# Two strips of counts in the third layer of a graph network, and 32 dense pairs with 40 gathered batches in its last two rounds

## The chip, the cores and the metric

The kernel runs on one core of one Trainium2 chip, in one launch. The metric is the device time of a launch in microseconds. Three runs of the kernel before took 5751.9, 5758.0 and 5763.0 us. The engines are named as in the profile: PE (matmuls), PEld (PE's loads of weights), DVE (vector), ACT (activation), POOL (GpSimd, which here issues the gathers of rows from DRAM) and SP (which issues the other transfers).

## The reference

Four graph layers follow each other on 6250 nodes of 128 features and one list of 106250 edges, sorted by the node `dst` that they end in; each layer adds its input and normalises the rows.

```python
x = ln(x + L0(x, src, dst, edge_type_16))   # two relational convolutions: means by (dst, relation), then a product
x = ln(x + L1(x, src, dst))                 # attention with a softmax over the edges of a node
x = ln(x + L2(x, src, dst, edge_type_8))    # below
x = ln(x + L3(x, src, dst))                 # below, twice

# L2: a relational layer, a residual product, and a norm over the nodes
agg = segment_sum(xW[src, etype], dst)
h = relu(agg + x @ loop_w + bias)
h = h + relu(x @ res_w + res_b)
out = (h - mean(h, 0)) * rsqrt(var(h, 0) + EPS) * bn_gamma + bn_beta

# L3: the mean of the neighbours, twice
def sage(x, W_l, W_r, b):
    return (segment_sum(x[src], dst) / max(degree, 1)) @ W_l.T + b + x @ W_r.T
out = sage(relu(sage(x, W1_l, W1_r, b1)), W2_l, W2_r, b2)
```

## The kernel before

The edges lie in 832 tiles of 128, and 8 tiles are a batch (104 batches). A round goes over all edges once: the first layer has two rounds, the second and third one each, the fourth two. In the gathering rounds POOL issues one indirect DMA for each tile, eight for a batch (`gather_near`, line 889, and `gather_mixed`, line 861), into a ring of four buffers. ACT copies the indices of a batch into one of four small buffers (`stage`, lines 1040 and 972); POOL waits for that copy, and ACT makes it when the batch four (in the last rounds three) before has been used.

The third layer's round (`near_round(near_c, ...)` on PE and DVE, `run_counting` on ACT) has 104 steps and one more, a batch each. In a step PE multiplies the gathered rows with one-hot matrices made by DVE (line 1491), ACT copies the sums out of PSUM (line 1065), PE multiplies them with the relations' weights one step later (line 1477), ACT copies again (line 1055), PE places the result (line 1501) and DVE adds it to the sums (line 2148).

Beside this the same round counts, for the fourth layer, how often each node is a source in each pair of batches. A pair d (0 to 29) is 16 tiles, of at most 128 target nodes; its counts are a strip of 128 partitions by 50 x 136 numbers in bf16, which is stored to DRAM (`neighbours`) when the pair is done. For a tile, DVE makes two one-hot matrices (lines 2023 for all of a step, 2029), PE multiplies them in two halves into two banks of PSUM (`count_tile`, line 1417), ACT takes them out into the strip at the tile's offset, all columns but the first (line 1034), and the first ones into a small buffer `SIDE` (line 1035), and DVE adds those to the strip (`correct`, line 2040). The banks are one set: PE begins a tile when ACT has taken out the one before. Five tiles are counted in a step (`PER`), three before and two beside the batch's own products; after 96 steps all pairs are counted. The loop's body is a lap of 16 steps, 5 pairs. There is one strip, `MADE_UP`. SP stores it when DVE's last correction is in (line 793), and ACT, before it takes out the first tile of the next pair, waits for that store:

```python
if j == 0:
    if not isinstance(d, int) or d > 0:
        act.wait_ge(made_out, d * 16)
```

The layer's residual product runs in the same round: 16 pieces of 400 columns, two in each lap and four behind the laps, a matmul (line 1702) and an activation into `H` (line 1266) each. After the round DVE waits for all of them (`res_act`) and goes on with `H`.

The last two rounds (`mixed_round`) use the counts. The first 60 batches, 30 pairs, are dense: SP loads a pair's strip into one of two buffers (line 798, when the products of the pair before the last are done), and PE multiplies it, 49 blocks of 128 nodes, with the rows of all nodes, held in SBUF as three bf16 parts (line 1710, 128x384 each); DVE adds up the three parts (line 2589), PE places the result (line 1756) and DVE adds it. The other 44 batches are gathered by POOL as before, and PE collects each in eight products (line 1780). The order of the work is written out: PE goes through half steps h, two for a pair (24 and 25 products), and a collect stands behind a half step that is a slot. Half steps 0 and 1 are the head, with a slot each; then a loop of four laps of 12 half steps (6 pairs), in which two of three half steps are slots (8 batches), and each half step also has a piece of the `x @ W_r` product (lines 1765, 1770); then the tail, 10 half steps (5 pairs), all of them slots. A pair whose tiles don't fit (more than 127 nodes in all, or steps from tile to tile above 11 nodes) takes another path, tile by tile (`wide`).

POOL issues the gathers in one loop from the moment the table of rows is stored, so ahead of PE by up to the ring's four buffers.

Of the kernel before, what the change touches and what calls it, by code (L numbers as in the profile page):

```python
# [22 lines left out]
ALU = mybir.AluOpType  # L23
# [59 lines left out]
def build(nc, a, out):  # L83
    ctx = ExitStack()
    with ctx:
# [237 lines left out]
        HOTS = PER  # L323
# [6 lines left out]
        MADE_UP = ROOM[:, 2 * NODES_P + R8 * P:2 * NODES_P + R8 * P + COUNTED].bitcast(BF16)  # L330
        MADE_HALVES = MADE_UP.rearrange("p (a h s) -> p a h s", a=2, s=STRIDE)
# [285 lines left out]
        def counted_in(lap, u):  # L617

            found = []
            for n in range(PER):  # L620
                q, j = divmod(PER * (u - 1) + n, PAIR)
                found.append((lap * PER + q, j))
            return found

        def offsets_of(engine, k):

            _, values = nc.values_load_multi_w_load_instructions(OFFSETS[0:1, bass.ds(k * PER - PER, PER)],
                                                                 engines=[engine.engine], min_val=0, max_val=LATEST,
                                                                 skip_runtime_bounds_check_because="VectorE clamps the offsets")
            return values  # L630
# [19 lines left out]
        def slot_before(lap, h):  # L650
# [4 lines left out]
            return lap * 2 + n // RING, n % RING  # L655

# [12 lines left out]
        def _(sp):  # L669
# [121 lines left out]
            with sp.Fori(0, DENSE) as d:  # L791
                sp.wait_ge(mx_cor, d * PAIR + PAIR)
                sp.dma_start(neighbours[bass.ds(d, 1), :, :].rearrange("o p s -> (o p) s"), MADE_UP).then_inc(made_out, 16)
# [139 lines left out]
        def _(act):  # L933
# [35 lines left out]
            def mixed_round(m, rows, final):  # L969
# [26 lines left out]
                with act.Fori(0, LAPS - 1) as lap:  # L996
# [20 lines left out]
            def take_out(d, j, n, offsets):  # L1017
# [13 lines left out]
                if j == 0:  # L1031
                    act.copy(MADE_HALVES[:, :, :, 0:SPAN], counted_of(2)).then_inc(mx_out, 1)
                else:
                    act.copy(MADE_HALVES[:, :, :, bass.ds(offsets[n] + 1, SPAN - 1)], counted_of(2)[:, :, :, 1:SPAN])  # L1034
                    act.copy(SIDE[:, n, :].rearrange("p (a h) -> p a h", a=2), counted_of(2)[:, :, :, 0]).then_inc(mx_out, 1)

            def near_round(r):
# [4 lines left out]
                def step(i, c, tiles=()):  # L1042
# [4 lines left out]
                    if tiles:  # L1047
                        offsets = offsets_of(act, k)
# [36 lines left out]
            def run_counting(step, residual):  # L1085

                def whole_lap(lap):
                    for u in range(1, COUNT_LAP + 1):
                        step(lap * (COUNT_LAP // FOUR) + u // FOUR, u % FOUR, counted_in(lap, u))
                        if u in RESIDUAL_AT:  # L1090
                            residual(lap * 2 + (RESIDUAL_AT.index(u) + 1))

# [170 lines left out]
            def residual(i):  # L1263

                act.wait_ge(res_pe, i + 1)
                act.activation(H[:, bass.ds((i - 1) * CHUNK, CHUNK)], PS[:, 7, 0:CHUNK], ACT.Relu, bias=vec("L2_gnn_res_b"))\
                    .then_inc(res_act, 1)
# [25 lines left out]
        def _(pe):  # L1293
# [117 lines left out]
            def count_tile(c, n, d, j):  # L1411
# [9 lines left out]
            def near_round(r, residual=None):  # L1421
# [36 lines left out]
                def step(i, c, tiles=()):  # L1458
# [37 lines left out]
                    if 1 <= now <= BATCHES:  # L1496
# [4 lines left out]
                        nc.tensor.matmul(PS[:, 5, 0:P], MADE[1 - b][:, :], PLACED[1 - b][:, :], start=True, stop=True).then_inc(placed, 1)  # L1501

                if residual:
                    step(0, 0)
                    with pe.Fori(0, COUNT_LAPS) as lap:
                        for u in range(1, COUNT_LAP + 1):
                            step(lap * (COUNT_LAP // FOUR) + u // FOUR, u % FOUR, counted_in(lap, u))
                            if u in RESIDUAL_AT:
                                residual(lap * 2 + (RESIDUAL_AT.index(u) + 1))
                    for n, k in enumerate(range(COUNTED_IN + 1, BATCHES + 1)):  # L1510
                        step(k // FOUR, k % FOUR)
                        if 2 * COUNT_LAPS + n < CHUNKS:
                            residual(2 * COUNT_LAPS + n + 1)
# [185 lines left out]
            def residual(i):  # L1699

                pe.wait_ge(res_act, i)
                nc.tensor.matmul(PS[:, 7, 0:CHUNK], mat("L2_gnn_res_w"), XF[:, bass.ds((i - 1) * CHUNK, CHUNK)],
                                 start=True, stop=True).then_inc(res_pe, 1)

            def mixed_round(m):
# [116 lines left out]
                with pe.Fori(0, LAPS - 1) as lap:  # L1822
                    for h in LAP_HALVES:
                        half_step(lap, h)
                for h in TAIL_HALVES:
                    half_step(LAPS - 1, h)
# [17 lines left out]
            pe.wait_ge(added, 3 * BATCHES)  # L1844
# [994 lines left out]
```

## Time and profile before

| | us |
|---|---|
| three runs: median (lowest to highest) | 5758.0 (5751.9 to 5763.0) |
| the profiled execution's own time | 5760.2 |
| its span, first to last instruction | 5758.3 |
| busy in the span: PE, PEld | 4169.4, 3454.7 |
| busy in the span: POOL, DVE, ACT | 3986.0, 2718.9, 1818.5 |
| the 832 gathers of the third layer's round | 3637 to 4746 |
| the 352 gathers of the fourth layer's first round | 4801 to 5242 |
| the 352 gathers of the fourth layer's second round | 5272 to 5714 |

Times in the profile count from the first instruction of one execution. A group of instructions is one line of the kernel on one engine with its operands; behind it stand the time that the engine was busy with it, the mean of one in ns, and the time that the engine stood idle just ahead of it, by what ended the idle time. "issue" there means that the profile shows nothing that was waited for; ACT IDX L1040 means the copy of a batch's indices. In a timeline, consecutive instructions of one line are one row, with the time from the first one's start to the last one's end; PE's matmuls overlap, so that such a row can reach a little past the start of the next. GB, ROOM, H and PACK are regions of SBUF that several buffers share, PS is PSUM.

### The profile page before, as it was taken

What the parts mean: (1) busy time and instruction counts of PE and PEld (TensorE: products, weight loads), DVE (VectorE), ACT (ScalarE), POOL (GpSimd) and SP (SyncE); (2) the same over time, 40 slices, a digit from 0 to 9 for tenths busy, and PEclk for the clock granted to TensorE, in tenths of its full rate; (3) what the DMA queues carried; (4) which work ended last, traced back from release to release, by engine and by line L of the source; (5) the groups of instructions that cost most, each with busy time, mean ns of one, the idle gap of its engine ahead of it and who ended that gap; (6) DMA issues with size and microseconds to landing.
All of it is one profiled execution on the core that took longest, in us unless ns stands there. A gap on an engine that the chain in (4) does not pass through costs nothing. (4 is left out here: it accounts for less than half of the span.)

```text
span 5758.3 us, 111258 instructions
## 1 busy us (share of the span) xinstructions
PE 4169.4 (72%) x25518; PEld 3454.7 (60%) x25519; DVE 2718.9 (47%) x10515; ACT 1818.5 (32%) x5132; POOL 3986.0 (69%) x4143
## 2 busy tenths in 40 slices
PE   4688888887777787656666668566665566886896
PEld 3577777776777776545555556454544454665664
DVE  8743333433333333256666666555555545334332
ACT  0122222222222222334444444544444442001001
POOL 3177777766777777377777775577777775776777
PEclk6699999999999999755666666888888888998998
DMA  3265656652222122133333332233333324554553
GB/s 87 48 171 153 162 153 163 157 147 60 52 52 52 52 52 52 44 88 85 87 84 87 85 86 70 74 102 101 98 99 107 104 88 142 188 178 137 189 187 111
DMA packets 380789, 609.48 MB, mean 106 GB/s; under 512 B 118627, under 2 KB 288132, under 8 KB 368516
## 3 DMA queue, kind: packets, MB, share of 16 engines
q1 hardware_dynamic: 246884, 331.68, 19.2%
q0 software_dynamic: 129024, 267.91, 18.4%
q8 instruction: 241, 3.95, 0.3%
q14 instruction: 512, 4.19, 0.2%
q10 hardware_dynamic: 4128, 1.75, 0.1%
HBM read 524.61 MB, written 76.38 MB: 104 GB/s over the span
## 5 line engine op out<-in xcount | busy, mean ns | idle before, releaser
L1477 PE MATMUL PS<-ROOM 128*128 128x128 f32 x8320 | 1046.4, 282 | 101.3 <-ACT ROOM L1065 99.8
L1477 PEld LDWEIGHTS PS<-ROOM 128*128 128x128 f32 x8320 | 989.1, 196 | 159.4 <-ACT ROOM L1065 109.3
L889 POOL DMA_INDIRECT GB<-table,IDX x832 | 801.3, 963 | 352.0 <-issue 247.8
L1065 ACT COPY ROOM<-PS 128x512 f32<-128x512 f32 x1040 | 609.4, 586 | 798.8 <-PE PS L1491 793.5
L889 POOL DMA_INDIRECT GB<-in_x,IDX x416 | 403.3, 969 | 296.8 <-ACT IDX L1040 157.0
L2148 DVE TENSOR_TENSOR ROOM<-ROOM,PS 128x128 f32 x312 | 89.7, 288 | 896.4 <-PE PS L1501 875.5
L889 POOL DMA_INDIRECT ROOM<-table,IDX x416 | 404.5, 972 | 137.5 <-issue 125.4
L849 POOL DMA_INDIRECT H<-table_gat,IDX x416 | 410.7, 987 | 126.8 <-issue 115.2
L849 POOL DMA_INDIRECT GB<-table_gat,IDX x416 | 406.0, 976 | 127.6 <-issue 125.6
L889 POOL DMA_INDIRECT H<-in_x,IDX x416 | 404.6, 973 | 126.8 <-issue 126.2
L889 POOL DMA_INDIRECT H<-table,IDX x416 | 396.8, 954 | 126.8 <-issue 122.5
L861 POOL DMA_INDIRECT GB<-table,IDX x352 | 335.0, 952 | 152.0 <-issue 105.8
L1635 PE MATMUL PS<-ROOM,OH 128*128 128x144 f32 x1664 | 428.0, 450 | 1.0 <-DVE RS L2376 1.0
L1491 PE MATMUL PS<-OH,GB 128*128 128x256 f32 (+1 forms) x1664 | 340.8, 359 | 119.6 <-DMA GB<-table,IDX 75.0
L861 POOL DMA_INDIRECT ROOM<-table,IDX x352 | 334.7, 951 | 107.3 <-issue 107.0
L1635 PEld LDWEIGHTS PS<-ROOM,OH 128*128 128x128 f32 x1664 | 395.1, 330 | 2.6 <-issue 1.0
L1491 PEld LDWEIGHTS PS<-OH,GB 128*128 128x128 f32 x1664 | 283.6, 210 | 165.3 <-issue 98.4
L1034 ACT CAST ROOM<-PS 128x550 f32 x450 | 299.1, 665 | 241.1 <-PE PS L1417 185.2
L2055 DVE SCALAR_TENSOR_TENSOR H<-iota_w,key,ROOM 128x256 f32<-128x256 f32 x416 | 173.8, 482 | 320.5 <-DVEq L2128 123.8
L1491 PE MATMUL PS<-OH,H 128*128 128x256 f32 x832 | 227.0, 434 | 95.9 <-DMA H<-in_x,IDX 55.1
L1710 PE MATMUL PS<-ROOM 128*128 128x384 bf16 x1470 | 263.4, 332 | 34.3 <-DVE ROOM L2581 33.1
L1710 PE MATMUL PS<-ROOM,PACK 128*128 128x384 bf16 x1470 | 270.6, 338 | 12.6 <-issue 11.8
(418 smaller groups left out, 7769.0 us busy)
## 6 DMA issues: line engine op xcount, KB each, us to landing
H<-one_over SPq DMA_DIRECT2D x416, 128.0 KB
ROOM<-one_over SPq DMA_DIRECT2D x416, 128.0 KB
neighbours<-ROOM SPq DMA_DIRECT2D x30, 1700.0 KB
ROOM<-neighbours SPq DMA_DIRECT2D x30, 1700.0 KB
PACK<-neighbours SPq DMA_DIRECT2D x30, 1700.0 KB
ROOM<-local_row SPq DMA_DIRECT2D x104, 256.0 KB
GB<-table,IDX POOLq DMA_INDIRECT x1184
ROOM<-table,IDX POOLq DMA_INDIRECT x768
```

The source lines that it names most:

```text
L849: pool.indirect_dma_start(out=out[:, j, :], out_offset=None, in_=r.table.dram[:, :], in_offset=bass.IndirectOffsetOnAxis(ap=idx[:, j:j + 1 ...
L861: pool.indirect_dma_start(out=RING_ROWS[c][:, j * P:(j + 1) * P], out_offset=None, in_=m.table.dram[:, :], in_offset=bass.IndirectOffsetOn ...
L889: pool.indirect_dma_start(out=r.rows[c][:, j * P:(j + 1) * P], out_offset=None, in_=r.dram[:, :], in_offset=bass.IndirectOffsetOnAxis(ap=I ...
L1034: act.copy(MADE_HALVES[:, :, :, bass.ds(offsets[n] + 1, SPAN - 1)], counted_of(2)[:, :, :, 1:SPAN])
L1065: act.copy(to.rearrange("p r (j d) -> p r j d", j=r.per), of.rearrange("p (j d r) -> p r j d", j=r.per, d=NEAR))\
L1477: ins = nc.tensor.matmul(PS[:, 4, 0:P], r.near[1 - b][:, t * P:(t + 1) * P], r.weights[:, t * P:(t + 1) * P], start=t == 0, stop=t == r.re ...
L1491: ins = nc.tensor.matmul(PS[:, n, j % r.per * r.cols:(j % r.per + 1) * r.cols], r.rows[c][:, j * P:(j + 1) * P], r.hot[b][:, j * r.cols:(j ...
L1635: ins = nc.tensor.matmul(PS[:, 1 - b, 0:MW_COLS], hot(1 - b)[:, j, :], MW[:, 1 - b, j, :], start=j == 0, stop=j == G - 1)
L1710: ins = nc.tensor.matmul(PS[:, bank, 0:3 * P], NEIGH[e][:, h, 0:P], XS[:, h, :], start=h == 0, stop=h == XBLOCKS - 1)
L2055: ins = dve.scalar_tensor_tensor(to, columns, key, WINDOWS[b][:, j * r.cols:(j + 1) * r.cols], ALU.is_equal, ALU.mult, accum_out=wstage[:, ...
L2148: dve.tensor_tensor(dst, dst, PS[:, 5, 0:P], ALU.add).then_inc(added, 1)
```

## The change

The constants: 32 dense pairs instead of 30, so 40 gathered batches instead of 44. A lap of the third layer's round is 12 steps and 4 pairs; a pair's 16 tiles are counted in three steps of 5, 5 and 6, the sixth behind the step's other work on PE and DVE. There are 8 laps, again 96 steps.

There are two strips: the second takes the upper 3400 columns of `H`, which the residual product doesn't reach until late. Even pairs use the one, odd pairs the other. ACT waits for the store of the pair before at tile 10 of a pair instead of at tile 0. Tile 0 is now taken out as the others are, with its first columns copied by DVE. DVE clears the second strip behind its step 0.

The residual product goes by columns: in each lap one piece of 350 columns (2800 in all, below the second strip), and behind the laps nine pieces of 400, two after the first step and one after each of the seven others. Ahead of these ACT waits for the stores of 31 pairs.

In the last two rounds the loop keeps its four laps, and the tail has 14 half steps (7 pairs) with six slots.

```diff
-LAP, LAPS = 6, 5
+LAP, LAPS = 6, 4
-DENSE = LAP * LAPS
+DENSE = 32
-PER, COUNT_LAP = 5, 16
-COUNT_LAPS = DENSE // PER
-COUNTED_IN = COUNT_LAP * COUNT_LAPS
-HEAD_HALVES, LAP_HALVES, TAIL_HALVES = range(0, 2), range(2, 2 + HALVES), range(2, HALVES)
-RESIDUAL_AT = [6, 14]
+HEAD_HALVES, LAP_HALVES, TAIL_HALVES = range(0, 2), range(2, 2 + HALVES), range(2, 2 * (DENSE - LAPS * LAP))
+TAIL_SLOTS = [2, 4, 7, 9, 12, 15]
+PER_LAP, LAP_OF = 4, 12
+COUNT_LAPS = DENSE // PER_LAP
+COUNTED_IN = LAP_OF * COUNT_LAPS
+TILES_OF = (range(0, 5), range(5, 10), range(10, 16))
+FREE_OF = [-5] * 5 + [-4] * 5 + [-4] * 6
+STORED_BY = 10
+RESIDUAL_AT, EARLY = 6, 350
+LATE_CHUNKS = (NODES_P - COUNT_LAPS * EARLY) // CHUNK
...
-        MADE_UP = ROOM[:, 2 * NODES_P + R8 * P:2 * NODES_P + R8 * P + COUNTED].bitcast(BF16)
+        MADE_UP = [H[:, NODES_P - COUNTED:NODES_P].bitcast(BF16),
+                   ROOM[:, 2 * NODES_P + R8 * P:2 * NODES_P + R8 * P + COUNTED].bitcast(BF16)]
...
+            q = (u - 1) // 3
+            return [(lap * PER_LAP + q, j, q % 2) for j in TILES_OF[(u - 1) % 3]]
...
-            return HEAD_HALVES if lap == 0 else TAIL_HALVES
+            return HEAD_HALVES if lap == 0 else TAIL_SLOTS
...
+        def late_chunks(k):
+            first = COUNTED_IN + 1
+            return (0, 1) if k == first else (k - first + 1,)
...
                 if j == 0:
+                    if isinstance(d, int) and d == 1:
+                        act.wait_ge(keyed, KEYED + 1)
+                if j == STORED_BY:
                     if not isinstance(d, int) or d > 0:
                         act.wait_ge(made_out, d * 16)
                         act.sem_inc(near_passed, 1)
-                if not isinstance(t, int) or t >= PER:
-                    act.wait_ge(mx_cor, d * PAIR + (j + 1 - PER))
+                if not isinstance(t, int) or FREE_OF[j] + t > 0:
+                    act.wait_ge(mx_cor, d * PAIR + (j + FREE_OF[j]))
...
-                if j == 0:
-                    act.copy(MADE_HALVES[:, :, :, 0:SPAN], counted_of(2)).then_inc(mx_out, 1)
-                else:
-                    act.copy(MADE_HALVES[:, :, :, bass.ds(offsets[n] + 1, SPAN - 1)], counted_of(2)[:, :, :, 1:SPAN])
-                    act.copy(SIDE[:, n, :].rearrange("p (a h) -> p a h", a=2), counted_of(2)[:, :, :, 0]).then_inc(mx_out, 1)
+                after = slice(1, SPAN) if j == 0 else bass.ds(offsets[n] + 1, SPAN - 1)
+                act.copy(MADE_HALVES[e][:, :, :, after], counted_of(2)[:, :, :, 1:SPAN])
+                act.copy(SIDE[:, n, :].rearrange("p (a h) -> p a h", a=2), counted_of(2)[:, :, :, 0]).then_inc(mx_out, 1)
...
-                for n, k in enumerate(range(COUNTED_IN + 1, BATCHES + 1)):
+                act.wait_ge(made_out, 16 * (DENSE - 1))
+                for k in range(COUNTED_IN + 1, BATCHES + 1):
                     step(k // FOUR, k % FOUR)
-                    if 2 * COUNT_LAPS + n < CHUNKS:
-                        residual(2 * COUNT_LAPS + n + 1)
+                    for n in late_chunks(k):
+                        residual(COUNT_LAPS + n, COUNT_LAPS * EARLY + n * CHUNK, CHUNK)
...
+                    for n in range(5, len(tiles)):
+                        count_tile(c, n, *tiles[n])
...
                 if j == 0:
-                    dve.sem_inc(mx_cor, 1)
+                    first = MADE_HALVES[e][:, :, :, 0:1].rearrange("p a h o -> p (a h) o")
+                    dve.tensor_copy(first, SIDE[:, n, :].unsqueeze(2)).then_inc(mx_cor, 1)
...
                     step(0, 0, (), counted_in(0, 1))
+                    dve.memset(MADE_UP[1], 0.0).then_inc(keyed, 1)
...
-                with pe.Fori(0, LAPS - 1) as lap:
+                with pe.Fori(0, LAPS) as lap:
                     for h in LAP_HALVES:
                         half_step(lap, h)
                 for h in TAIL_HALVES:
-                    half_step(LAPS - 1, h)
+                    half_step(LAPS, h)
...
-            dve.wait_ge(res_act, 1 + CHUNKS)
+            dve.wait_ge(res_act, 1 + COUNT_LAPS + LATE_CHUNKS)
```

## Rows read from the trace of the kernel before

**Rows 1.** page, engines' busy time, and shares of the chain that ended last

```profile
PE 4169.4 (72%) x25518; PEld 3454.7 (60%) x25519; DVE 2718.9 (47%) x10515; ACT 1818.5 (32%) x5132; POOL 3986.0 (69%) x4143
...
POOL 8%; issue 3%; PE 2%; DVE 0%; DMA 0%; POOLq 0%; DVEq 0%; ACT 0%; SPq 0%; ACTq 0%
```

**Rows 2.** groups of POOL's instructions, 3650 to 4750 us: busy, mean ns, idle before

```profile
L889 POOL DMA_INDIRECT ROOM<-table,IDX x416 | 404.5, 972 | 137.5 <-issue 125.4 <-ACT IDX L1040 12.1
...
L889 POOL DMA_INDIRECT GB<-table,IDX x407 | 395.4, 972 | 159.7 <-issue 118.9 <-ACT IDX L1040 40.8
```

**Rows 3.** timeline of POOL, third layer's round: start us, us, instruction, idle before it

```profile
3637.38 1.08 POOL L889 DMA_INDIRECT GB<-table,IDX  x1 [28.91 <-ACT IDX L1040]
```

**Rows 4.** waits, 3660 to 4700 us: total us, times, longest

```profile
ACT ROOM L1032 <- DMA neighbours<-ROOM: 210.2, 24, 10.7
```

**Rows 5.** timeline, 3960 to 4030 us

```profile
3964.14 0.37 DVE L2029 TENSOR_SCALAR PACK<-iota_h,key 128x600 bf16<-128x600 f16 x1
...
3974.53 0.66 ACT L1032 CAST ROOM<-PS 128x600 bf16<-128x600 f32 x1 [8.76 <-DMA neighbours<-ROOM]
...
3984.52 0.42 PE L1417 MATMUL PS<-PACK,SPARE 128*128 128x300 bf16 x2 [0.51 <-ACT SPARE L1035]
...
3992.65 0.42 PE L1417 MATMUL PS<-PACK 128*128 128x300 bf16 x2 [0.86 <-ACT SPARE L1035]
```

**Rows 6.** groups of POOL's instructions, 4798 to 5250 us

```profile
L861 POOL DMA_INDIRECT ROOM<-table,IDX x176 | 167.2, 950 | 53.6 <-issue 53.3 <-ACT IDX L972 0.3
```

**Rows 7.** timeline of POOL, start of the fourth layer's first round

```profile
4800.61 0.98 POOL L861 DMA_INDIRECT GB<-table,IDX  x1 [15.56 <-DMA table<-X]
```

**Rows 8.** timeline of PE, end of the fourth layer's first round

```profile
5150.75 4.07 PE L1710 MATMUL PS<-ROOM,PACK 128*128 128x384 bf16 x24
...
5154.66 0.38 PE L1756 MATMUL PS<-sel_first,same 128*128 128x128 f32 x2
...
5157.65 2.05 PE L1780 MATMUL PS<-OH,ROOM 128*128 128x128 f32 x16 [2.61 <-DMA ROOM<-table,IDX]
...
5159.54 4.23 PE L1710 MATMUL PS<-ROOM,PACK 128*128 128x384 bf16 x25
...
5163.60 1.95 PE L1780 MATMUL PS<-OH,ROOM 128*128 128x128 f32 x16
...
5247.19 3.78 PE L1780 MATMUL PS<-OH,ROOM 128*128 128x128 f32 x16 [5.25 <-DMA ROOM<-table,IDX]
```

**Rows 9.** timeline, end of the third layer's round

```profile
4704.19 0.84 PE L1702 MATMUL PS<-ROOM,PACK 128*128 128x400 f32 x2
...
4705.07 0.59 ACT L1266 ACTIVATE H<-PS,vecs 128x400 f32<-128x400 f32 x1 [0.22 <-PE PS L1702]
```

**Rows 10.** timeline of PE, end of the fourth layer's second round

```profile
5620.78 4.07 PE L1710 MATMUL PS<-ROOM,PACK 128*128 128x384 bf16 x24
...
5627.93 3.68 PE L1780 MATMUL PS<-OH,ROOM 128*128 128x128 f32 x16 [2.86 <-DMA ROOM<-table,IDX]
...
5631.44 4.23 PE L1710 MATMUL PS<-ROOM,PACK 128*128 128x384 bf16 x25
...
5668.40 0.38 PE L1756 MATMUL PS<-sel_first,same 128*128 128x128 f32 x2
...
5668.62 1.95 PE L1780 MATMUL PS<-OH,ROOM 128*128 128x128 f32 x16
...
5670.41 4.23 PE L1710 MATMUL PS<-ROOM,PACK 128*128 128x384 bf16 x25
...
5716.84 3.60 PE L1780 MATMUL PS<-OH,ROOM 128*128 128x128 f32 x16 [3.32 <-DMA ROOM<-table,IDX]
```

**Rows 11.** timeline of SP, fourth layer's first round

```profile
5163.93 0.33 SPq L798 DMA_DIRECT2D PACK<-neighbours  x1
```

**Rows 12.** windows: busy us (x) by engine, PEclk, DMA share, GB/s

```profile
5171.00:5172.00 1.00, 0.00 (x0) 0.00 (x0) 0.00 (x0) 0.00 (x0) 0.70 (x2) 1.00 0.33 86
```

**Rows 13.** timeline of PE, first lap's end in the third layer's round

```profile
3834.59 0.66 PE L1417 MATMUL PS<-PACK,SPARE 128*128 128x300 bf16 x2 [10.72 <-issue]
```

More of the change, by code:

```diff
@@ L617, in counted_in, with offsets_of @@
         def counted_in(lap, u):
[L619 to L627, printed above, removed]
+            q = (u - 1) // 3
+            return [(lap * PER_LAP + q, j, q % 2) for j in TILES_OF[(u - 1) % 3]]
+        def offsets_of(engine, tiles):
+            d, j, _ = tiles[0]
+            _, values = nc.values_load_multi_w_load_instructions(OFFSETS[0:1, bass.ds(d * PAIR + j, len(tiles))],
                                                                  engines=[engine.engine], min_val=0, max_val=LATEST,
@@ L789, in store_rows, with store_counts @@
                     sp.dma_start(t.dram[columns_of(g), :].rearrange("(n p) f -> p n f", p=P), rows).then_inc(t.stored[0], 16)
-            with sp.Fori(0, DENSE) as d:
+            def store_counts(d, e):
                 sp.wait_ge(mx_cor, d * PAIR + PAIR)
-                sp.dma_start(neighbours[bass.ds(d, 1), :, :].rearrange("o p s -> (o p) s"), MADE_UP).then_inc(made_out, 16)
+                sp.dma_start(neighbours[bass.ds(d, 1), :, :].rearrange("o p s -> (o p) s"), MADE_UP[e]).then_inc(made_out, 16)
+            with sp.Fori(0, DOUBLES) as i:
+                for e in range(2):
+                    store_counts(2 * i + e, e)
             def load(m, d, e):
@@ L995, in mixed_round @@
                     half_step(0, h)
-                with act.Fori(0, LAPS - 1) as lap:
+                with act.Fori(0, LAPS) as lap:
                     for h in LAP_HALVES:
@@ L1087, in whole_lap @@
                 def whole_lap(lap):
[L1088 to L1091, printed above, removed]
+                    for u in range(1, LAP_OF + 1):
+                        step(lap * (LAP_OF // FOUR) + u // FOUR, u % FOUR, counted_in(lap, u))
+                        if u == RESIDUAL_AT:
+                            residual(lap, lap * EARLY, EARLY)
                 step(0, 0)
@@ L1261, in _, with residual @@
                                bias=vec("L2_gnn_bias")).then_inc(begin_sb, 1)
[L1263 to L1267, printed above, removed]
+            def residual(n, column, width):
+                act.wait_ge(res_pe, n + 2)
+                act.activation(H[:, bass.ds(column, width)], PS[:, 7, 0:width], ACT.Relu, bias=vec("L2_gnn_res_b")).then_inc(res_act, 1)
             stage, step = near_round(near_c)
@@ L1505, in near_round @@
                     with pe.Fori(0, COUNT_LAPS) as lap:
[L1506 to L1510, printed above, removed]
+                        for u in range(1, LAP_OF + 1):
+                            step(lap * (LAP_OF // FOUR) + u // FOUR, u % FOUR, counted_in(lap, u))
+                            if u == RESIDUAL_AT:
+                                residual(lap, lap * EARLY, EARLY)
+                    for k in range(COUNTED_IN + 1, BATCHES + 1):
                         step(k // FOUR, k % FOUR)
-                        if 2 * COUNT_LAPS + n < CHUNKS:
-                            residual(2 * COUNT_LAPS + n + 1)
+                        for n in late_chunks(k):
+                            residual(COUNT_LAPS + n, COUNT_LAPS * EARLY + n * CHUNK, CHUNK)
                     return
@@ L2168, in near_round @@
                     step(0, 0, (), counted_in(0, 1))
+                    dve.memset(MADE_UP[1], 0.0).then_inc(keyed, 1)
                     with dve.Fori(0, COUNT_LAPS) as lap:
-                        for u in range(1, COUNT_LAP + 1):
-                            step(lap * (COUNT_LAP // FOUR) + u // FOUR, u % FOUR, counted_in(lap, u), counted_in(lap, u + 1))
+                        for u in range(1, LAP_OF + 1):
+                            step(lap * (LAP_OF // FOUR) + u // FOUR, u % FOUR, counted_in(lap, u), counted_in(lap, u + 1))
                     for k in range(COUNTED_IN + 1, BATCHES + 1):
@@ L2738, in mixed_round @@
                     half_step(0, h)
-                with dve.Fori(0, LAPS - 1) as lap:
+                with dve.Fori(0, LAPS) as lap:
                     for h in LAP_HALVES:
```

60 lines of the change are left out of this document (31 added, 29 removed).

## The prediction

> **What bounds the kernel now.** I read the page first: POOL is busy 69% of the span and is also the engine on which the chain of waits ends, with 8% of the span on the gathers of line 861 [rows 1]. The shares of the chain add up to some 13% of the span: it reaches back into the last two rounds only and says nothing of the third layer's. So the question for each round is whether POOL ever stops between its gathers. Three rounds are touched, and I read POOL's groups with the idle time ahead of them in each.
>
> In the third layer's round POOL issues 832 gathers of 972 ns with 0.30 us between two of them, and beside that it was held 12.1 + 40.8 = 52.9 us by ACT's copy of the next indices [rows 2]. It starts at 3637.4 [rows 3]. So the round is almost POOL's, but not quite: something slows ACT. The waits of the round name it: ACT stood 210 us, in 24 waits of up to 10.7 us, on the store of the strip of counts to DRAM [rows 4]. One such wait is seen closely: ACT idle for 8.76 us on the store; some steps later, with no store in the way, one whole step of five counted tiles on PE goes from 3984.52 to 3992.65, 8.13 us [rows 5]. A gather batch takes 8 x (0.972 + 0.302) = 10.19 us. A pair (3.2 steps) therefore takes 3.2 x 8.13 + 8.8 = 34.8 us by the counting chain and 32.6 us by POOL: counting is the slower by about 2 us, and the difference comes out as POOL's 52.9 us.
>
> In the last two rounds POOL has no idle time except the 0.30 us between gathers (53.3 us over 175 of them), with gathers of 950 ns [rows 6]. A batch there is 8 x (0.950 + 0.304) = 10.03 us, and 44 of them are a round, 441 us, the first from 4800.6 on [rows 7]. PE has the time to follow: at the end of the first round its last collect starts only when the DMA lands, 5.25 us idle [rows 8].
>
> **The change, part by part.** *Strips.* Pair d + 1 now counts into the other strip, so ACT asks for the store of pair d - 1 only at tile 10 of pair d. That is about two steps, 16 to 20 us, after the store was issued; the wait seen was 8.8 us from strip to strip [rows 5], so it is over by then. The wait is gone, and what is late next is POOL itself: the step of five tiles is 8.13 us, and of six tiles 8.13 + 8.13/5 = 9.76 us, so a lap of twelve steps is 8 x 8.13 + 4 x 9.76 = 104.1 us on PE and ACT against 122.3 us of POOL. The 52.9 us shrink to the 0.30 us that each of these 31 gathers would have had anyway: gain 52.9 - 9.3 = 43.6 us. Bounds: 0, if the counting chain still holds the round, and 43.6; below 0 only by what rival (c) says.
>
> *Two more pairs to count.* 32 tiles more, on PE, ACT and DVE, all inside that slack. On POOL they could cost through DVE: gathers average 972 ns beside the counting [rows 2] and 950 without it [rows 6], 18 us over 832 for 480 tiles, so 32 more cost about 1.2 us. The Trainium skill (SBUF — State Buffer, Who interferes with whom) says that a DVE operation in a two-port mode shuts GpSimd out for its whole length, so that descriptors are not written. One compare of the counting is 0.37 us [rows 5]; by that rule in full, 480 of them cost POOL up to 178 us and 32 more up to 12 us, which would make the sum 11 us larger. The trace agrees with the direction and not with the size.
>
> *Residual product.* Eight pieces of 350 columns lie inside laps (nothing on the path); nine of 400 columns now follow the last steps, the last one behind the last step. Its product is 0.84 us, the activation 0.59 us and starts 0.22 us after [rows 9]. DVE waits for all of them before it goes on, while its own last addition runs beside: I take 1.3 us, and 0.5 us for the piece ahead of step 104 which stands on PE while that engine is on the path: 1.8 us; between 0.5 and 3. The memset of the second strip stands behind DVE's first step, where DVE waits for the first gathers; nothing. The round: -43.6 + 1.2 + 1.8 = -40.6 us.
>
> *40 batches, 32 pairs.* The head and the four laps of the loop are the same as before: 34 batches and 25 pairs. Only the straight part behind the loop changes: ten half steps with a batch each become fourteen half steps with six. POOL saves 4 x 10.03 = 40.1 us a round. But the last half steps now have more PE work per batch, so I walk PE through them. A first half is 24 products, 3.91 us (5150.75 to 5154.66); a second half 25, 4.06 us (5159.54 to 5163.60) [rows 8]; a placing 0.22 us and a collect that doesn't wait 1.79 us [rows 10]. Nothing differs until the first collect of that part is over: 5159.54 in the first round, 5631.44 in the second. From there: seven second halves 28.4, six first halves with their placing 24.8, five collects 9.0, in sum 62.2 us, which ends at 5221.7 and 5693.6. Do the batches arrive in time? The last one is issued by 4800.6 + 401.2 = 5201.8, and lands some 5.2 us later by the last collect of before (issued by 5242.0, begun at 5247.19): 5207, while PE comes to it at 5219.9. The one that comes closest is batch 35, at about 5167 when PE asks at 5167.7. So PE, not POOL, now ends the round. Before, the last collect began at 5247.19 and 5716.84 and was slow after its wait, 3.78 and 3.60 us instead of 1.95 [rows 8, 10]. Gain 27.3 + 1.8 = 29.1 and, with the last collect begun at 5691.8, 25.0 + 1.7 = 26.7 us: 55.8 together. Bounds: 20 a round (some 8 us more of waits on PE) and 40.1 (POOL's own saving).
>
> Two covers could fail there. The pairs' loads: a strip's next load is issued when its products are done (5163.93 [rows 11]); the DMA is back at the gathers' own rate at 5171 [rows 12], so 7 us, and the other pair's products and a collect lie between, 10 us: hidden, with 3 us to spare. The index buffers: a batch is staged when the fourth before it is collected; the last gather starts its batch 30 us after that. Hidden. If a load is late each time by 2 us, the round loses 10 us.
>
> **Sum.** The profiled execution took 5760.2 us (span 5758.3), 2.2 above the median of the runs and inside their 5751.9 to 5763.0. 5760.2 - 40.6 - 55.8 = 5663.8; against the median it is 5661.6. I say 5663.
>
> **The rivals.**
> (a) *POOL ends the last rounds too*: PE is faster there than walked, and the whole 40.1 us comes, twice. 5760.2 - 40.6 - 80.2 = 5639. For it: before, POOL set the end. Against: 57 us of products and 11 of collects are more than 60 us of gathers.
> (b) *The third layer's round keeps its pace*: the counting chain is the bound even without the store, because what the store's wait hid is now in the open. Every lap starts with a pause of PE, 10.72 us, of which the profile names nothing [rows 13]; it lies at the same place as a store wait, since a lap begins with a pair, so it cost nothing of its own. There are eight laps now, and six before. On PE: 104.1 + 10.7 + 0.8 for the residual is 115.6 of 122.3 us, which fits, and POOL is up to three batches ahead, which cushions it. If it doesn't fit, only the last rounds gain: 5760.2 - 55.8 = 5704. The Trainium skill (Runtime: NRT & Kernel Launch, Instruction fetch mechanics) says that instructions are fetched ahead in order and that a taken branch to code no longer held stops the engine until it is fetched. That would be this pause, and by it the eight laps speak against the change; the row has its size.
> (c) *Slower*: the same place, further. ACT, PE and DVE each branch back, and each could pause on its own, one after the other, as they wait for each other in turn. A lap is POOL's until the pauses are 17.4 us; each us beyond costs 8. Pauses of 23 us eat the 43.6 us of this round (8 x 5.5), and at 30 us a lap, three times the one seen, the 55.8 us of the last rounds are gone too: 5663.8 + 8 x (30 - 17.4) = 5765, and 5805 at 35. Against: in the trace the three engines' pauses at a lap's start fit into one of 10.7.
> (d) *The new pairs leave the short path*: a pair whose 16 tiles span more than 127 nodes, or step by more than 11, goes tile by tile through eleven counts and 49 products each. By 1.63 us a count (8.13/5) and 0.163 us a product that is 26 us a tile, 414 us a pair and round: 5664 + 830 = 6490 for one pair. The reference's drawn edges give pairs 30 and 31 spans of 120 and 119 nodes and steps of at most 9, so this hardly can be.
>
> **How the numbers follow.** The forecast 0.78 with its own range of 5645 to 5685 (the residual 3 us dearer, loads late, or PE at full speed behind the tail a little quicker); (a) 0.06; (b), wholly or in part (5685 to 5706), 0.12; (c) and (d) 0.04. The range that leaves out 2 in 10 at most: from (a) to (b), 5638 to 5703. About 0.2%, 11 us, is what a measurement here tells from no change. The cases but (c) and (d) are all faster by more: faster 0.95, same 0.01, slower 0.04.
>
> **What would show it.** Right: no wait of ACT on the store in the third layer's round, or a few us; POOL's idle time on the index copy there under 15 us, and the round's gathers within 1068 us from first to last; in the two last rounds 320 gathers each with 0.30 us between, and behind the last one PE still at products for 15 to 20 us, its last collect without a wait on DMA. Wrong: POOL waiting for index copies at lap starts (b, c); a last collect that waits for its gather (a); PE idle on the loads of the strips in the last seven pairs; more than 49 products a pair (d).

## The result, and the profile after

The changed kernel takes 5669.5 us (median of 4 runs, 5661.6 to 5675.7), the kernel before 5758.8 in the same session: a ratio of 0.9846 (95% interval, here and below in brackets: [0.9831, 0.9862]), 89 us less. The forecast was 5663. The profiled execution of the changed kernel took 5668.5 us (span 5666.6) against 5760.2, so by the profiles the sum to account for is 91.7 us, where 96.4 were forecast. Cut at events that both traces show (the first and the last gather of a round, and the 98 products behind a round, L1839 before and L1855 after), it falls apart so:

| stretch | before, us | after, us | change | forecast |
|---|---|---|---|---|
| up to the third layer's first gather | 3637.4 | 3637.8 | +0.5 | 0 |
| third layer's round, first to last gather | 1108.8 | 1068.4 | -40.4 | -43.6 + 1.2 |
| from there to the next round's first gather | 54.5 | 55.8 | +1.3 | +1.8 |
| last rounds, the first: first gather to the products behind it | 452.0 | 424.8 | -27.2 | -29.1 |
| from these products to the next first gather | 19.3 | 17.9 | -1.4 | 0 |
| last rounds, the second, likewise | 449.9 | 423.4 | -26.5 | -26.7 |
| from there to the end | 36.6 | 38.6 | +2.0 | 0 |

The page of the changed kernel, which answers to [rows 1]: POOL's share of the chain that ended last has gone down from 8% to 5%, PE's up from 2% to 3%.

```profile
PE 4176.6 (74%) x25660; PEld 3443.9 (61%) x25661; DVE 2739.9 (48%) x10550; ACT 1845.4 (33%) x5219; POOL 3929.4 (69%) x4079
...
POOL 5%; PE 3%; issue 2%; DMA 0%; DVE 0%; POOLq 0%; ACT 0%; DVEq 0%; SPq 0%; ACTq 0%
```

*Third layer's round.* First POOL's groups of the changed kernel from 3650 to 4750 us (busy, mean ns | idle before and what ended it), which answer to [rows 2]:

```profile
L902 POOL DMA_INDIRECT ROOM<-table,IDX x416 | 406.3, 977 | 126.8 <-issue 126.2 <-ACT IDX L1054 0.6
L902 POOL DMA_INDIRECT GB<-table,IDX x408 | 399.8, 980 | 124.3 <-issue 124.3
```

Of the 12.1 + 40.8 us that POOL stood for ACT's index copy 0.6 are left, and in the list of ACT's waits in this round there is none on a DMA any more, where [rows 4] had 210.2 us. But the mean of a gather has gone from 972 to 977 and 980 ns. Two windows, from the first to the last gather, show both at once. The columns are the busy time and the number of instructions of PE, PE's weight loads, DVE, ACT and POOL, then clock, DMA share and GB/s. The kernel before:

```profile
3637.38:4746.15 1108.77, 673.70 (x4492) 552.15 (x4492) 561.12 (x2067) 517.73 (x1355) 809.21 (x832) 0.85 0.32 99
```

and the changed one:

```profile
3637.83:4706.23 1068.40, 691.68 (x4554) 559.78 (x4554) 592.62 (x2162) 544.90 (x1448) 815.15 (x832) 0.89 0.34 106
```

POOL's time between gathers is 1108.8 - 809.2 = 299.6 us before and 253.3 after, a gain of 46.3; the same 832 gathers took 5.9 us more.

*Last rounds.* The timeline of PE in the changed kernel, at the end of both of these rounds (start us, us, instruction, idle before it), answers to [rows 8, 10]:

```profile
5119.78 3.64 PE L1796 MATMUL PS<-OH,ROOM 128*128 128x128 f32 x16 [2.85 <-DMA ROOM<-table,IDX]
5123.26 4.23 PE L1726 MATMUL PS<-ROOM,PACK 128*128 128x384 bf16 x25
...
5183.56 1.95 PE L1796 MATMUL PS<-OH,ROOM 128*128 128x128 f32 x16
5185.35 0.39 PE L1772 MATMUL PS<-sel_last,slots 128*128 128x128 f32 x2
...
5563.40 4.26 PE L1726 MATMUL PS<-ROOM,PACK 128*128 128x384 bf16 x25
...
5624.53 1.95 PE L1796 MATMUL PS<-OH,ROOM 128*128 128x128 f32 x16
5626.32 0.39 PE L1772 MATMUL PS<-sel_last,slots 128*128 128x128 f32 x2
```

and the timeline of POOL, the first and the last gather of the first of them and the first of the next:

```profile
4762.00 0.99 POOL L874 DMA_INDIRECT GB<-table,IDX  x1 [16.84 <-DMA table<-X]
...
5162.54 0.94 POOL L874 DMA_INDIRECT ROOM<-table,IDX  x1 [0.30 <-issue]
5204.70 0.94 POOL L874 DMA_INDIRECT GB<-table,IDX  x1 [41.22 <-DMA table<-H]
```

Behind the first collect of the tail PE has no wait of more than 0.7 us: from 5123.26 to 5185.35 are 62.1 us and from 5563.40 to 5626.32 are 62.9, where the walk gave 62.2. The last collect doesn't wait, and POOL had issued its last gather 20 us before it.

A collect is eight products, 16 instructions in the profile. The first of the tail took 3.64 us and the last 1.95, for the same work. Two windows over them, with the columns as above, show why: the first ran at a granted clock of 0.52 of full, close to the lower of TensorE's two levels (1.2 GHz), after PE had stood for 2.85 us; the last ran at 1.00 (2.4 GHz), straight behind other products.

```profile
5119.78:5123.26 3.48, 3.48 (x17) 3.47 (x18) 0.00 (x0) 0.00 (x0) 2.61 (x3) 0.52 0.24 57
5183.56:5185.35 1.79, 1.79 (x19) 1.79 (x18) 0.75 (x2) 0.00 (x0) 0.00 (x0) 1.00 0.67 122
```

### The profile page after: what moved, and what is told of

Same layout as the page of the kernel before. It is cut to its first block and busy times, and to the rows that moved or that the text cites. A ratio compares the mean times of both kernels' runs of the same rounds, so it can differ in the third digit from the quotient of the medians.

```text
span 5666.6 us, 111492 instructions
## 1 busy us (share of the span) xinstructions
PE 4176.6 (74%) x25660; PEld 3443.9 (61%) x25661; DVE 2739.9 (48%) x10550; ACT 1845.4 (33%) x5219; POOL 3929.4 (69%) x4079
## 5 line engine op out<-in xcount | busy, mean ns | idle before, releaser
L902 POOL DMA_INDIRECT GB<-table,IDX x832 | 805.7, 968 | 316.4 <-issue 252.9
L902 POOL DMA_INDIRECT ROOM<-table,IDX x416 | 406.3, 977 | 126.8 <-issue 126.2
L1651 PE MATMUL PS<-ROOM,OH 128*128 128x144 f32 x1664 | 424.8, 447 | 1.3 <-DVE RS L2396 1.3
L874 POOL DMA_INDIRECT GB<-table,IDX x320 | 304.9, 953 | 155.0 <-issue 96.3
L874 POOL DMA_INDIRECT ROOM<-table,IDX x320 | 304.8, 953 | 97.5 <-issue 97.2
L1726 PE MATMUL PS<-ROOM 128*128 128x384 bf16 x1568 | 279.0, 331 | 34.0 <-DVE ROOM L2601 33.0
L1726 PE MATMUL PS<-ROOM,PACK 128*128 128x384 bf16 x1568 | 286.6, 337 | 14.2 <-issue 12.3
L1198 ACT ACTIVATE OH<-iota_w,local 128x128 f32<-128x128 f32 x832 | 254.4, 388 | 69.6 <-PE PS L1616 69.6
```

The costliest lines, as they stand in the source:

```text
L874: pool.indirect_dma_start(out=RING_ROWS[c][:, j * P:(j + 1) * P], out_offset=None, in_=m.table.dram[:, :], in_offset=bass.IndirectOffsetOn ...
L902: pool.indirect_dma_start(out=r.rows[c][:, j * P:(j + 1) * P], out_offset=None, in_=r.dram[:, :], in_offset=bass.IndirectOffsetOnAxis(ap=I ...
L1198: ins = act.activation(hot(b)[:, j, :], iota_f[:, :], ACT.Abs, bias=local[:, bass.ds(k * G + j, 1)], scale=-1.0)
L1651: ins = nc.tensor.matmul(PS[:, 1 - b, 0:MW_COLS], hot(1 - b)[:, j, :], MW[:, 1 - b, j, :], start=j == 0, stop=j == G - 1)
L1726: ins = nc.tensor.matmul(PS[:, bank, 0:3 * P], NEIGH[e][:, h, 0:P], XS[:, h, :], start=h == 0, stop=h == XBLOCKS - 1)
```

## The experiments

Each time is a median beside runs of the kernel before on the same chip, or a single run where that is said; a small difference between two experiments is read from the stretches of the table, which differ less from execution to execution than the whole.

**The parts by themselves.** The last two rounds of before, behind the third layer's round of after:

```
-SPARSE = BATCHES - 2 * DENSE
+PAIRS = 30
+SPARSE = BATCHES - 2 * PAIRS     # and PAIRS for DENSE all through the last two rounds
-TAIL_SLOTS = [2, 4, 7, 9, 12, 15]
+TAIL_SLOTS = TAIL_HALVES
```

> The third layer's round is that of the change (two strips, 32 pairs counted, the residual in laps), but the last two rounds are those of before: 30 dense pairs, 44 gathered batches, so pairs 30 and 31 are counted and not used. If the two parts add up as the trace of the change says (26.8 us of gain in each of the last two rounds): near 5722, that is 37 less than before, about the 40.4 of the third layer's round less 1.3 behind it. If the third layer's gain were only a matter of this one execution, or the strips helped the last rounds as well: over 5735 or under 5710.

Measured 5725.1 us, 0.9946 [0.9929, 0.9962] of before: 29.8 us less in the same session, where 37 were expected, with an interval from 22 to 41. By the trace its third layer's round took 1070.2 us, and the last rounds 452.5 and 451.1, as before. Within that interval the two parts add up.

**One strip.** 

```
-        MADE_UP = [H[:, NODES_P - COUNTED:NODES_P].bitcast(BF16), ROOM[...].bitcast(BF16)]
+        MADE_UP = [ROOM[...].bitcast(BF16)] * 2
-STORED_BY = 10
+STORED_BY = 0
```

(The clearing of the second strip is left out as well.)

> The changed kernel with one strip of counts instead of two, so that ACT again asks for the store at the first tile of each pair. Theory: that wait is what held the index copies. A pair then takes 16 x 1.63 + 8.8 = 34.9 us on the counting chain while POOL's three batches take 30.6: 4.3 us for each of 31 pairs, less some 30 us that POOL is ahead at most, so 100 to 133 us slower, 5770 to 5803, with POOL waiting for index copies by that much. Rival: the gain came from the new layout of laps (three steps to a pair, four pairs to a lap) or from fewer residual pieces, and the strip has little to do with it: under 5690.

Measured 5744.7 us, 0.9982 [0.9972, 0.9992] of before: 75 us slower than with two strips. The round took 1148.1 us instead of 1068.4. ACT's wait on the store, and POOL's groups:

```profile
ACT ROOM L1047 <- DMA neighbours<-ROOM: 177.7, 23, 9.0
```

```profile
L901 POOL DMA_INDIRECT GB<-table,IDX x416 | 409.8, 985 | 195.2 <-issue 121.3 <-ACT IDX L1053 73.9
L901 POOL DMA_INDIRECT ROOM<-table,IDX x416 | 407.8, 980 | 164.2 <-issue 132.0 <-ACT IDX L1053 32.3
```

Of the 73.9 us some 29 are the wait ahead of the first gather, which every version has; the other 45 and the 32.3 are the round's loss. So the strip is the cause, and with one strip the new layout of laps, three steps to a pair with two pairs more, makes this round 39 us slower than before. The size was guessed too high: a wait is 7.7 us on the mean (177.7 / 23), not 8.8, and there are 23 of them, not 31. At the lap's start at 3927 ACT waited 10.42 us for PE, and not for the store.

**When the store is asked for.** `STORED_BY = 10` to `STORED_BY = 5`.

> Two strips, but ACT asks for the store of the pair before at tile 5 instead of tile 10, one step (8 to 10 us) after the store was issued instead of two. A store was waited for 7.7 us on the mean with one strip. Theory (only the moment of asking counts, and a step covers the store): waits of ACT on the store of 0 to 2 us each, POOL without waits for index copies, 5669 within 6. Rival: the store takes longer beside the next pair's work, and some 3 us a pair come back: POOL waits some tens of us, over 5685.

Measured 5666.8 us (one run), and no wait of ACT on a DMA in the round. POOL's groups are those of the changed kernel:

```profile
L902 POOL DMA_INDIRECT GB<-table,IDX x416 | 408.2, 981 | 155.5 <-issue 126.5 <-ACT IDX L1054 29.0
L902 POOL DMA_INDIRECT ROOM<-table,IDX x416 | 405.8, 976 | 126.8 <-issue 126.1 <-ACT IDX L1054 0.6
```

In this run one step covers the store; the two that the change leaves are more than it needs.

**What sets the end of the last rounds.** Four kernels change only the order there. The theory that I had formed from the trace of after (A) says that PE is the bound from its first product on: in the first of these rounds it waited 4.7 us for gathers, and 28.4 us for nothing that the trace names. The waits of PE, changed kernel, 4762 to 5186 us (total us, times, longest):

```profile
PE PS L1726 <- issue: 12.3, 3, 4.5
PE PS L1781 <- issue: 8.9, 3, 3.5
PE PS L1796 <- issue: 7.2, 1, 7.2
...
PE PS L1796 <- DMA ROOM<-table,IDX: 4.7, 2, 2.9
```

Fewer laps:

```
-LAP, LAPS = 6, 4
+LAP, LAPS = 12, 2                # slot_at and slot_before: lap * (LAP // 3) for lap * 2
```

> The last two rounds' loop runs 2 laps of 12 pairs instead of 4 laps of 6, the order of all work unchanged. Theory A (PE is the bound of these rounds from its first product on: in the first one it runs from 4769.49 to 5185.35 and waits 4.7 us for gathers in all; the 21.2 us that it stands at three lap starts for no reason that the trace names are on the path): two of the three pauses go, 14.2 us a round; the last gather, landed at about 5168.7, then binds, so 13 us a round, 26 in all, near 5643. Theory B (the prediction's: POOL sets the pace up to the first collect of the tail, and what PE loses in a lap is hidden): no change, 5669 within 6. Theory C (the pause is paid by length of code, not by branch): no change or slower, with pauses of PE inside the lap.

Measured 5666.3 us, 0.9845 [0.9832, 0.9859]. PE's waits in the first of these rounds:

```profile
PE PS L1796 <- DMA ROOM<-table,IDX: 13.4, 5, 3.4
PE PS L1796 <- issue: 7.4, 1, 7.4
...
PE PS L1726 <- issue: 4.8, 3, 2.8
PE PS L1781 <- issue: 4.3, 1, 4.3
```

The pauses shrank by 11.9 us (two of about 7.1 are gone, and 2.0 us of new ones stand inside the longer laps), the waits for gathers grew by 8.7, and the round (first gather to the products) went from 424.8 to 422.0 us. So theory A falls: in the laps POOL sets the pace, as the prediction had it, but with next to no room. The long pauses belong to the branch back: with three branches there were three, with one there is one. Most of their length was not on the path. The Trainium skill (Runtime: NRT & Kernel Launch, Instruction fetch mechanics) says that a taken branch to code outside what is held stalls the engine until that code is fetched; the place of the pauses agrees, and no run here shows the fetch itself.

Two pairs ahead of the loop:

```
-HEAD_HALVES, LAP_HALVES, TAIL_HALVES = range(0, 2), range(2, 2 + HALVES), range(2, ...)
+HEAD_HALVES, LAP_HALVES, TAIL_HALVES = range(0, 6), range(6, 6 + HALVES), range(6, ...)
+HEAD_SLOTS, TAIL_SLOTS = [1, 5], [6, 8, 10, 12, 13, 15]
...
```

> Two of the pairs of the straight part behind the loop are done ahead of it, beside the same two first batches: ten half steps instead of fourteen behind the loop. Theory B (only PE's work behind the loop counts): 16.4 us less there, until the last gather binds, so 13 us a round, 26 in all, near 5643. Theory A (PE is the bound all along, so work that is only moved stays on the path): at most its waits for gathers, 4.7 us, and the slow collect behind one, 1.6 us, go: 0 to 6 us a round, 5657 to 5669. A third way: the fifth batch's indices come later, POOL stalls at the start, and the round is longer: over 5675.

Measured 5658.8 us, 0.9824 [0.981, 0.9837]; the rounds took 415.4 and 416.0 us, 9.4 and 7.3 less. Neither size was right. In the first one PE waits for no gather any more (4.7 us), its pauses sum to 24.8 us (3.6 less), and the slow collect is gone (1.6): 9.9 in sum, about the 9.4, since now PE is the bound from its first product to its last. And POOL, held up at the start by index copies that come later, needed 404.9 us for its gathers instead of 401.5 (its timeline):

```profile
4821.92 0.94 POOL L879 DMA_INDIRECT GB<-table,IDX  x1 [0.96 <-ACT IDX L990]
4833.33 0.94 POOL L879 DMA_INDIRECT ROOM<-table,IDX  x1 [1.73 <-ACT IDX L990]
```

Collects late, `TAIL_SLOTS = [5, 7, 9, 11, 13, 15]`:

> The six collects of the part behind the loop stand behind half steps 5, 7, 9, 11, 13 and 15 instead of 2, 4, 7, 9, 12 and 15. Both theories: PE no longer waits there for a gather (2.85 us in the first round, 3.35 in the second) nor runs the collect after it slowly (3.64 instead of 1.95 us): 4.6 to 5 us a round, 9 to 10 in all, near 5660. If the later collects hold up the index copies and so POOL: 5669 or more.

Measured 5660.9 us, 0.9834 [0.982, 0.9847]; 420.5 and 419.4 us, 4.3 and 3.9 less. Collects early, `TAIL_SLOTS = [2, 3, 5, 6, 8, 15]`:

> The six collects of the part behind the loop stand behind half steps 2, 3, 5, 6, 8 and 15. Walked with a batch every 10.03 us, halves of 4.06 and 4.13 us and collects of 3.6 us after a wait: PE waits for four more gathers and ends at 5193.7 instead of 5185.4 in the first round, 8.3 us later, 17 in both, near 5686. If the order of the collects doesn't matter, because POOL's own pace or the adding on DVE sets the end: 5669.

Measured 5687.9 us, 0.9884 [0.9869, 0.9899]; 431.2 and 431.7 us, 6.4 and 8.3 more. PE waits again in the tail:

```profile
5119.15 3.79 PE L1796 MATMUL PS<-OH,ROOM 128*128 128x128 f32 x16 [3.40 <-DMA ROOM<-table,IDX]
...
5146.94 2.05 PE L1796 MATMUL PS<-OH,GB 128*128 128x128 f32 x16 [2.93 <-DMA GB<-table,IDX]
```

For the late collects the walk of PE was right in size and in way. For the early ones the size came out to 2 us, but not by the way that was expected: PE waits for one more gather in the tail of each round (2.93 and 3.91 us), not for four. In the first round the rest is mostly the 25 products behind the slow collect, which took 5.41 us instead of 4.23 since the granted clock was still 0.77 on the mean there, and 1.0 us that PE stood ahead of two later half steps, 0.79 of it for DVE. That the sum fitted is in part luck.

**A better version.** PE and POOL are nearly balanced in these rounds, so an edit to one of them gains until the other binds. Three such edits together: one pair ahead of the loop (`HEAD_SLOTS = [1, 3]`), two laps of 12 pairs, collects at 6, 8, 10, 12, 13 and 15.

> Three of the earlier changes of order in one kernel: one pair of the straight part done ahead of the loop, two laps of 12 pairs, and the collects behind the loop placed late (half steps 6, 8, 10, 12, 13 and 15). If PE and POOL are equally bound in these rounds, so that each alone gave 3 to 10 us and lost the rest to the other engine: all of PE's slack is used now and POOL binds, its 401.5 us of gathers and the 10.4 us that followed the last one where PE waited for it, 412 us from the first gather to the products behind the round (424.8 and 423.4 in the changed kernel): 11 to 13 us a round, 5644 to 5648. If the gains are of the same waits and don't add up: near 5659, as with two pairs ahead of the loop.

Measured 5638.5 us (5631.8 to 5640.6), 0.9797 [0.9784, 0.981] of before and 31 us under the changed kernel. The rounds took 408.1 and 409.3 us, 30.8 less in sum. Alone, by the same two rounds, two laps gave 4.3, two pairs ahead 16.7 and late collects 8.2, 29.2 in all (by the medians of the whole 3, 11 and 9): the gains about add up, though only one pair is ahead here. POOL and PE at the end of the first one:

```profile
5160.79 0.94 POOL L879 DMA_INDIRECT ROOM<-table,IDX  x1 [0.30 <-issue]
```

```profile
5165.44 2.05 PE L1801 MATMUL PS<-OH,ROOM 128*128 128x128 f32 x16
5167.33 0.39 PE L1777 MATMUL PS<-sel_last,slots 128*128 128x128 f32 x2
5168.77 3.50 PE L1860 MATMUL PS<-turned,ROOM 128*128 128x128 f32 x29 [1.05 <-DVE ROOM L2684]
```

The gathers took 401.1 us and the products began 7.0 behind the last one: PE comes to its last collect, without a wait, 4.7 us after the last gather was issued, so the two end nearly together. I had expected 10.4, from rounds in which PE stood before the last collect and ran it in 3.6 to 3.8 us; here it comes straight from other products and takes 2.05.

**What slows the gathers of the third layer's round.** Is the 971 ns of before stable at all? The kernel before again, unchanged:

> The kernel before, unchanged, profiled a second time. Gathers of the third layer's round had a mean of 971 ns in its first profile and 978 to 984 in the profiles of the changed kernel's round. If that is a property of the kernel: 971 again, within 2. If it differs from execution to execution: anything from 968 to 985, and then the 7 us of gathers that the change seemed to cost there are not shown.

Measured 5755.6 us (one run), mean 970.7 ns over the round's 832 gathers; seven profiles whose round is that of the changed kernel have 978 to 984. The two profiles of before and these seven don't overlap, so the difference belongs to the kernel. POOL's waits are those of the first profile too: 69.5 less the 29 of the start, and 13.1.

```profile
L889 POOL DMA_INDIRECT GB<-table,IDX x416 | 406.1, 976 | 191.1 <-issue 121.6 <-ACT IDX L1040 69.5
L889 POOL DMA_INDIRECT ROOM<-table,IDX x416 | 403.0, 969 | 137.6 <-issue 124.5 <-ACT IDX L1040 13.1
```

Three suspects, each doubled. The stores:

```
+                sp.dma_start(again[bass.ds(d, 1), :, :]..., MADE_UP[e]).then_inc(made_out, 16)
```

> Each strip is stored twice, the second time to another place in DRAM: 54 MB more over the third layer's round. If the drag on the gathers (0.980 us with the stores and the counting, 0.953 without) is the DMA traffic of the stores: a mean near 1.0 us, 15 to 20 us more over the round. If it is VectorE or else: 0.980. Whether the store is still early enough at tile 10 shows too: a wait of ACT on it, which is absent with one store.

5673.4 us (one run), mean 982.3 ns, inside the spread, and still no wait of ACT on a store. Not the stores. The key compares, one tensor operand from SBUF each:

```
+                dve.tensor_scalar(HOT_KEY[n], iota_h[:, :], near_col[:, column], None, ALU.is_equal)
                 dve.tensor_scalar(HOT_KEY[n], iota_h[:, :], near_col[:, column], None, ALU.is_equal)
```

> Every key compare of the counting is done twice on VectorE: 512 more operations of 0.37 us, 190 us of them. If such a compare shuts POOL out for its whole length: up to 190 us more of gathers in the third layer's round, a mean near 1.2 us each instead of 0.980. If what drags the gathers is only some of it, as the 28 ns on 832 gathers (23 us for all counting) say: at most 23 us more, a mean of 0.98 to 1.01. If the drag has nothing to do with the compares: 0.980, no change. The round itself grows by that or by what the longer counting chain adds.

5719.1 us (one run). The gathers are no slower, 974 ns on the mean; what the time went into is the counting chain, which now holds POOL by its index copies, while PE waits for the compares:

```profile
L902 POOL DMA_INDIRECT ROOM<-table,IDX x416 | 406.3, 977 | 146.7 <-issue 122.6 <-ACT IDX L1054 24.1
L902 POOL DMA_INDIRECT GB<-table,IDX x416 | 405.2, 974 | 191.6 <-issue 119.7 <-ACT IDX L1054 71.8
```

```profile
PE PS L1431 <- DVE PACK L2050: 162.1, 67, 6.7
```

The wide compare of a step, which reads two operands from SBUF:

```
+                dve.tensor_tensor(HOT_LO[c % 2][:, 0:m, :], mid(iota_h[:, 0:P], m), ...)
                 dve.tensor_tensor(HOT_LO[c % 2][:, 0:m, :], mid(iota_h[:, 0:P], m), ...)
```

> VectorE's wide compare of a step (one for the low bits of five or six tiles, 0.87 us on the mean, 96 in the round) is done twice. In the changed kernel 102 of 764 gathers of the round took over 1.02 us, and 44% of these ran beside that compare, against 18% of all. If it is this compare that holds up POOL: some 45 more long gathers, about 0.25 us each, a mean of 0.99 instead of 0.978 and 11 us more of gathers. If it only stands where something else is slow, or the count of compares doesn't matter: 0.978 within 0.004. The longer counting chain may also bring back waits of POOL for index copies; these are read apart.

5684.1 us (one run). Mean 996 ns: 828.7 us of gathers against 813.8 in the changed kernel, both summed over the timeline, and no new wait for index copies:

```profile
L902 POOL DMA_INDIRECT GB<-table,IDX x416 | 416.8, 1002 | 155.3 <-issue 125.5 <-ACT IDX L1054 29.7
L902 POOL DMA_INDIRECT ROOM<-table,IDX x416 | 413.1, 993 | 126.8 <-issue 125.5 <-ACT IDX L1054 1.2
```

So 96 more such compares cost POOL 15 us (10 against the slowest of the seven), 0.11 to 0.16 us for each of 0.87 us. The unedited kernels agree: in the trace of before the 148 gathers of this round that ran beside a wide compare took 1061 ns on the mean and the other 684 took 951; in the changed kernel 139 took 1076 and the other 693 took 958.

## Why the prediction was right, and where its sizes were off

*Strips: 43.6 forecast, 46.3 measured.* The 2.7 us more are mostly five gaps of POOL, up to 1.9 us, for which the trace of before names nothing and which are gone too. The mechanism was right in each link: with one strip ACT's wait on the store and POOL's waits for index copies come back, with two both are gone, also when the store is asked for a step earlier. Rivals (b) and (c) fall: PE still pauses at a lap's start, up to 10.9 us, and POOL doesn't notice.

*More gathers dragged: 1.2 forecast, 5.9 measured.* This is the term that was mis-sized most. I spread the whole drag over the counted tiles and took it as in proportion to them. The runs show a drag by the two-operand compare, and none in the mean by the key compare, which was the operation that I had priced by the two-port rule of the Trainium skill (SBUF — State Buffer, Who interferes with whom). The same section of the Trainium skill says that a DVE instruction with two inputs from SBUF contends with what GpSimd reads there; that is the sentence that this case agrees with, though a compare costs POOL only 12 to 18% of its length. Why the changed kernel, with the same 96 wide compares (a third of them a fifth longer), loses 5.9 us stays open: most of it lies in the 693 gathers that ran beside no wide compare, 7 ns on each. The kernel with one strip loses as much (mean 981 ns), so it isn't the second strip. That the round as a whole came within 2 us is in part luck: the strips gave 2.7 us more than forecast, the drag cost 4.7 more.

*Residual: 1.8 forecast, 1.3 measured.* Within its bounds; the figure is the whole stretch behind the round, and the residual was not changed by itself.

*Last rounds: 29.1 and 26.7 forecast, 27.2 and 26.5 measured.* The walk of PE behind the first collect of the tail was right to 1 us, and rival (a) fell: POOL was 23 us ahead of the products behind the first round. What was off by 2.3 us is the starting point of the first round. I took it as unchanged, 358.9 us behind the first gather; it came at 361.3 (5123.26 - 4762.00). PE waits there for its gather in both kernels (2.61 us before [rows 8], 2.85 after); the collect began 0.7 us later, and it ran in 3.64 us instead of 2.05, at a granted clock of 0.52 instead of 1.00. Placing the collects later takes that away. Rival (d) fell: 3136 products are 49 for each of 64 pairs.

*Not in the sum:* the 98 products between the rounds took 11.21 us instead of 12.79. Before, they came behind a collect that had waited 5.25 us, and their first 3 us ran at a granted clock of 0.50; now they run at 1.00 throughout, as behind the second round of before, where they also took 11.21. And the end came 2.0 us later: the last store to the output, issued at 5661.12, ended the span 5.5 us on, where it was 3.5 before. All kernels with 32 pairs in the last rounds have this, those with 30 don't; why was not looked into.

What I missed was not in the forecast but beside it: that PE and POOL are nearly balanced in the laps as well, so that the same pairs and batches in another order were worth another 31 us.

## What to carry to other kernels

When an engine off the path waits for a store, a second buffer is worth the wait only down to the pace of the next engine (here 210 us of ACT's waits were worth 46 us); find the pace of both over the whole period, and check it in the waits of the engine that feeds the bound. When work is moved from the bound engine to another, walk the other one instruction by instruction to the end of the stage: the end changes hands. Where two engines are within some per cent of each other, an edit to one gives only the room that the other leaves (two laps: pauses 11.9 us shorter, the round 2.8); try such edits together before any is dropped.

## What the runs showed of the hardware

- A VectorE compare with two operands in SBUF (128 x 640 or 768, 0.87 us) lengthens the issue of GpSimd's indirect DMAs by 0.11 to 0.16 us; 512 more compares with one tensor operand (0.39 us) didn't lengthen it (974 ns on the mean, 978 without them). One run each.
- A pause of PE at the branch back of the last rounds' loop, 7.1 us (21.2 in three), goes when the lap goes. In the third layer's round the pause at a lap's start is up to 10.9 us; there the laps were not changed by themselves.
- The 16 instructions of a collect take 1.95 to 2.05 us behind other products, at a granted clock of 1.00. Behind a wait they can take up to 3.79: in the kernel before 3.68 us behind a wait of 2.86, at 0.51, and 3.78 behind 5.25, at 0.50, but 2.05 behind 2.61, at 1.00.
- Behind a pause at the branch back the first 12 products of 128x384 take 4.02 us, at 0.50, and 2.11 in the middle of a lap.
